# First edge pass of a graph network: 26 columns by one-hots and sixteen landed rows, in place of 34 and eight

## What is computed

```python
h = maximum(layernorm(x), 0)
nq = concatenate([h, query_embedding for every node], -1)
q, k = nq @ Wq + bq, nq @ Wk + bk
v = h @ Wv + bv
rel = relation_embeddings[edge_type]                 # 64 types
scores = sum(q[dst] * (k[src] + rel), over a head) / sqrt(16)
exp_s = exp(scores - max(segment_max(scores, dst), 0)[dst])
out = segment_sum(exp_s / (segment_sum(exp_s, dst) + 1e-8)[dst] * v[src], dst)
x = x + out @ Wo + bo
```

## Time and profile before

| | us |
|---|---|
| median of 3 runs | 8171.97 (8163.74 to 8175.19) |
| profiled execution | 8224.43 |
| its span | 8222.7 |
| first gather of the pass to last landed-value product | 1229.7 to 3020.07 |

### The profile page before, as it was taken

The page is one execution under the profiler, slowest core; times in us unless marked ns, Lnnn a source line. Parts: engine busy times, 40 slices in busy tenths (PEclk is TensorE's granted clock), DMA queues, the critical chain, the costliest instruction groups (busy, mean ns, idle before and its releaser), DMA issues. The chain is left out here.

```text
span 8222.7 us, 115102 instructions
## 1 busy us (share of the span) xinstructions
PE 3022.9 (37%) x29723; PEld 2454.6 (30%) x29724; DVE 4813.4 (59%) x11169; ACT 1435.3 (17%) x3773; POOL 3490.1 (42%) x3926
## 2 busy tenths in 40 slices
PE   4189423445566652244323432344300000001344
PEld 3178312344455542233223432333200000000122
DVE  9658835556566555677556875677544444444333
ACT  0123100111111121222112221344411111110000
POOL 0100113333323324456445653544466665563655
PEclk9999955667677675667666676666655555555666
DMA  0023203333323333334433453334322222222334
GB/s 20 10 85 100 51 27 100 80 92 88 85 69 83 77 60 68 79 80 87 64 75 80 82 82 61 72 80 72 57 48 53 52 52 50 46 50 54 78 82 78
DMA packets 297357, 557.19 MB, mean 68 GB/s; under 512 B 137694, under 2 KB 182475, under 8 KB 280515
## 3 DMA queue, kind: packets, MB, share of 16 engines
q0 software_dynamic: 112432, 254.18, 20.4%
q1 hardware_dynamic: 146802, 260.29, 10.0%
q10 hardware_dynamic: 38049, 41.86, 1.7%
HBM read 459.57 MB, written 29.32 MB: 59 GB/s over the span
## 5 line engine op out<-in xcount | busy, mean ns | idle before, releaser
L2967 PE MATMUL bank<-tab,oh 128*128 128x136 bf16 x11700 | 895.5, 249 | 695.4 <-PEq L2959 406.5
L2967 PEld LDWEIGHTS bank<-tab,oh 128*128 128x128 bf16 x11700 | 866.2, 112 | 755.5 <-issue 755.5
L1382 PE MATMUL bank<-ident,hid 128*128 128x128 f32 x125 | 55.8, 446 | 2651.0 <-PEq L1381 1182.8
L1382 PEld LDWEIGHTS bank<-ident,hid 128*128 128x128 f32 x125 | 22.7, 182 | 2697.7 <-issue 2697.7
L2710 POOL DMA_INDIRECT land_a<-table,idx_a x624 | 680.2, 1090 | 228.9 <-issue 166.4
L2729 POOL DMA_INDIRECT land_r<-table,idx_r x492 | 495.8, 1008 | 215.6 <-issue 144.4
L2546 PE MATMUL bank<-tab_l,oh_l 128*128 128x128 bf16 x3846 | 446.8, 243 | 289.2 <-issue 230.7
L2890 ACT ACTIVATE rows<-bank 128x408 f32<-128x408 f32 x936 | 398.5, 513 | 854.3 <-ACTq L2889 639.5
L2816 DVE TENSOR_TENSOR prod<-prod 128x128 f32<-128x128 f32 (+4 forms) x621 | 536.8, 864 | 14.6
L2519 PE MATMUL bank<-rel_l,oht_l 128*128 128x128 bf16 x3222 | 436.8, 261 | 245.4 <-issue 124.6
L2802 DVE TENSOR_TENSOR prod<-rows,bank 128x5376 f32<-128x5376 f32 x75 | 431.6, 5755 | 53.5 <-DVEq L2801 30.6
(11 more groups left out here) (506 smaller groups left out, 8264.3 us busy)
## 6 DMA issues: line engine op xcount, KB each, us to landing
loc<-el_loc SPq DMA_DIRECT2D x78, 1088.0 KB
loc_l<-el_loc SPq DMA_DIRECT2D x52, 1088.0 KB
rows_r<-land_r SPq DMA_DIRECT2D x123, 272.0 KB
landings_l<-landings_l SPq DMA_DIRECT2D x41, 784.0 KB
attr<-in_edge_attr ACTq DMA_DIRECT2D x75, 343.8 KB
land_a<-table,idx_a POOLq DMA_INDIRECT x936
typ_l<-el_typ SPq DMA_DIRECT2D x52, 192.0 KB
land_r<-table,idx_r POOLq DMA_INDIRECT x492
```

Source lines behind the costliest of these rows:

```text
L2967: last = pe.matmul(got[g % full][:, (c - of[0]) * W1:(c - of[0] + 1) * W1], oh[:, o], tab[:, t, x], start=n == 0, stop=n == len(parts) - 1 ...
```

## The change

The eight wide columns are no longer made by TensorE: their table rows, whose indices now stand in the stored list ahead of the overflow slots, are gathered by GpSimd. FC = 26 columns stay with the one-hots, LAND = 16 are landed. The key groups become four landed, two narrow of four columns and six narrow of three; the twelve value groups cover 26 columns in twos and threes. The relation types are loaded in two pieces in the order of the columns. The stored list is eight entries longer, and the later passes read it at an offset. The overflow turns keep their slots.

```diff
--- before
+++ after
@@ -148,7 +148,7 @@
-        el_ovf = dram("el_ovf", [RMAX + 1, P, 2 * LISTW], I32)
+        el_ovf = dram("el_ovf", [RMAX + 1, P, NW + 2 * LISTW], I32)
@@ -1249,7 +1249,7 @@
-                sp.dma_start(el_ovf[bass.ds(r + n, 1)].rearrange("r p s -> p (r s)"), ov_i[:, PC:]).then_inc(s("el_stored"), 16)
+                sp.dma_start(el_ovf[bass.ds(r + n, 1)].rearrange("r p s -> p (r s)"), ov_i[:, PC - NW:]).then_inc(s("el_stored"), 16)
@@ -2035,19 +2035,21 @@
-assert MC % 2 == 0
+FC = NB + 1
+LAND = MC - FC
+assert MC % 2 == 0 and LAND == NW + FIRST
...
-run_idx, run_now = bb("run_idx", [P, 2 * LISTW], I32), bb("run_now", [P, 2 * LISTW], I32)
-idx_a, idx_r = bb("idx_a", [P, FIRST], I32), bb("idx_r", [P, 2, MORE], I32)
-loc, typ = bb("loc", [P, PC * P], F16), bb("typ", [P, TH * P], F16)
-oh, oht = bb("oh", [P, OHC, P], BF16), bb("oht", [P, TH, P], BF16)
+run_idx, run_now = bb("run_idx", [P, NW + 2 * LISTW], I32), bb("run_now", [P, NW + 2 * LISTW], I32)
+idx_a, idx_r = bb("idx_a", [P, LAND], I32), bb("idx_r", [P, 2, MORE], I32)
+loc, typ = bb("loc", [P, FC * P], F16), bb("typ", [P, TH * P], F16)
+oh, oht = bb("oh", [P, FC, P], BF16), bb("oht", [P, TH, P], BF16)
...
-land_a, va = bb("land_a", [P, FIRST, W0]), bb("va", [P, FIRST, HV])
+land_a, va = bb("land_a", [P, LAND, W0]), bb("va", [P, LAND, HV])
@@ -2061,21 +2063,18 @@
-wide = [range(c, min(c + 4, PC)) for c in range(NB + 1, PC, 4)]
 narrow = [range(c, c + 4) for c in range(NB - 7, NB + 1, 4)] + [range(c, c + 3) for c in range(0, NB - 7, 3)]
-landed_groups = [range(PC + c, PC + c + HALF) for c in range(0, FIRST, HALF)]
-key_groups = landed_groups + wide + narrow
-value_groups = [range(max(c - BANKC, 0), c) for c in range(PC, 0, -BANKC)]
+landed_groups = [range(c, c + HALF) for c in range(FC, MC, HALF)]
+key_groups = landed_groups + narrow
+VG = 2 * len(banks)
+value_groups = [range(FC * (n - 1) // VG, FC * n // VG) for n in range(VG, 0, -1)]
 AHEAD = len(banks)
-type_halves = [[(9, 18), (30, MC)], [(0, 9), (18, 30)]]
-type_place = {}
-for k, pieces_of in enumerate(type_halves):
-    of_half = [c for a0, a1 in pieces_of for c in range(a0, a1)]
-    type_place.update({c: (k, i) for i, c in enumerate(of_half)})
+type_place = {c: (c // TH, c % TH) for c in range(MC)}
...
-assert sorted(c for of in value_groups for c in of) == list(range(PC))
+assert sorted(c for of in value_groups for c in of) == list(range(FC))
+assert all(len(of) <= BANKC for of in value_groups)
@@ -2105,14 +2104,12 @@
-            sp.dma_start(loc[:], el_loc[bass.ds(r, 1), 0:PC].rearrange("r j p -> (r j p)").partition_broadcast(P)).then_inc(s("loc_in"), 16)
+            sp.dma_start(loc[:], el_loc[bass.ds(r, 1), 0:FC].rearrange("r j p -> (r j p)").partition_broadcast(P)).then_inc(s("loc_in"), 16)
...
-            for k, pieces_of in enumerate(type_halves):
-                for a0, a1 in pieces_of:
-                    at = type_place[a0][1]
-                    sp.dma_start(typ[k * TYPES:(k + 1) * TYPES, at * P:(at + a1 - a0) * P],
-                                 el_typ[bass.ds(r, 1), a0:a1].rearrange("r j p -> (r j p)").partition_broadcast(TYPES)).then_inc(s("typ_in"), 16)
+            for k in range(2):
+                sp.dma_start(typ[k * TYPES:(k + 1) * TYPES],
+                             el_typ[bass.ds(r, 1), k * TH:(k + 1) * TH].rearrange("r j p -> (r j p)").partition_broadcast(TYPES)).then_inc(s("typ_in"), 16)
@@ -2158,9 +2155,9 @@
-            pool.tensor_copy(idx_a[:], run_idx[:, 0:FIRST]).then_inc(ch.semaphore, ch.one())
+            pool.tensor_copy(idx_a[:], run_idx[:, 0:LAND]).then_inc(ch.semaphore, ch.one())
             copied()
-            for c in range(FIRST):
+            for c in range(LAND):
@@ -2177,7 +2174,7 @@
-                    pool.tensor_copy(idx_r[:], run_now[:].rearrange("p (k s) -> p k s", k=2)[:, :, bass.ds(i * MORE + FIRST, MORE)]).then_inc(ch.semaphore, ch.one())
+                    pool.tensor_copy(idx_r[:], run_now[:, NW:].rearrange("p (k s) -> p k s", k=2)[:, :, bass.ds(i * MORE + FIRST, MORE)]).then_inc(ch.semaphore, ch.one())
@@ -2208,8 +2205,8 @@
-            dve.wait_ge(s("typ_in"), 64)
-            dve.sem_inc(s("typ_in"), -64)
+            dve.wait_ge(s("typ_in"), 32)
+            dve.sem_inc(s("typ_in"), -32)
@@ -2218,10 +2215,7 @@
-            dve.tensor_scalar(oh[:, 0:PC].rearrange("p c n -> p (c n)"), loc[:], iota_p[:], None, ALU.is_equal).then_inc(ch.semaphore, ch.one())
-            for k in range(1, WIDE):
-                dve.tensor_scalar(oh[:, PC + (k - 1) * NW:PC + k * NW].rearrange("p c n -> p (c n)"), loc[:, (NB + 1) * P:],
-                                  iota_k[:, k:k + 1], None, ALU.is_equal).then_inc(ch.semaphore, ch.one())
+            dve.tensor_scalar(oh[:].rearrange("p c n -> p (c n)"), loc[:], iota_p[:], None, ALU.is_equal).then_inc(ch.semaphore, ch.one())
@@ -2322,7 +2316,7 @@
-            dve.tensor_tensor(by_head(kp[:, PC:]), by_head(va[:]), wt[:, PC:MC].unsqueeze(3).broadcast_to([P, FIRST, HEADS, V]), ALU.mult).then_inc(ch.semaphore, ch.one())
+            dve.tensor_tensor(by_head(kp[:, FC:]), by_head(va[:]), wt[:, FC:MC].unsqueeze(3).broadcast_to([P, LAND, HEADS, V]), ALU.mult).then_inc(ch.semaphore, ch.one())
@@ -2406,7 +2400,7 @@
-            act.wait_ge(s("got_a_l0"), r * (16 * FIRST) + 16 * FIRST)
+            act.wait_ge(s("got_a_l0"), r * (16 * LAND) + 16 * LAND)
@@ -2522,22 +2516,22 @@
-                if of[0] >= PC:
+                if of[0] >= FC:
...
-                    done = pe.matmul(keys_of(n), ident[:], land_a[:, of[0] - PC:of[0] - PC + HALF, 0:D],
+                    done = pe.matmul(keys_of(n), ident[:], land_a[:, of[0] - FC:of[0] - FC + HALF, 0:D],
                                      start=False, stop=True, skip_group_check=True)
-                    if n == 1:
+                    if n == len(landed_groups) - 1:
...
-                        pe.sem_inc(s("bank_full1"), 1)
+                        pe.sem_inc(s(f"bank_full{n}"), 1)
                     else:
-                        done.then_inc(s("bank_full0"), 1)
+                        done.then_inc(s(f"bank_full{n}"), 1)
@@ -2647,7 +2641,7 @@
-            sp.dma_start(run_idx[:], el_ovf[bass.ds(r, 1), :, 0:LISTW].rearrange("r p s -> p (r s)")).then_inc(s("list_in"), 16)
+            sp.dma_start(run_idx[:], el_ovf[bass.ds(r, 1), :, NW:NW + LISTW].rearrange("r p s -> p (r s)")).then_inc(s("list_in"), 16)
```

## The result

After the change the kernel takes **8311.12 us** (median of 4 runs, 8294.45 to 8319.74), beside 8173.58 for the kernel before in the same series: ratio 1.0168, 95% interval 1.015 to 1.0186, slower by 137.5 us where I forecast 69. The profiled execution of after (8309.06, span 8307.3) lies at its median; that of before lay 52 above its own. The loss is in this pass.

A forecast was written before the change was run, and what follows sets the result against it. TensorE's issue was taken to be nearly stopped while gathers are in flight in the first edge pass. Fourteen single-turn intervals +21, two-turn +20, longer ones and the first +20, one more +8: +69 on 8172, 8241 us; range 8140 to 8320.

The forecast's parts named there:

- the pricing of the interval: First edge pass, per interval between landed-value products: +1.5 us with one overflow turn, +4 with two, +4 with three to five.
- 1.3 us of VectorE's time booked as saved: Behind the keys: VectorE's value groups take 4.3 us for 26 columns instead of 5.68 for 34.
- Rival A: First gathers do not lengthen TensorE's slow stretch; single-turn late keys end before 48.9; -209 us, 7963; chance 0.13.
- C: Late keys all pass at 3.6 per us and the values are covered: +5 us, no change; chance 0.14.
- D: As C, plus a stock of queued matmuls when the late keys start: -32 us, 8140; chance 0.07.
- B: The poorer pace, 0.9 matmuls per us, holds throughout the stretch under gathers: +151 us, 8323; chance 0.16.
- The pace of the late keys in the stretch: TensorE, single-turn interval: 3.6 per us under first gathers, 2.3 or 0.9 under overflow gathers, leaving 37 to 54 matmuls.
- The 2.5 us saved behind the keys: Single-turn interval after the last keys: 1.3 us from fewer value columns and 1.2 us from smaller one-hots.
- The longer intervals: Two-turn intervals: +4 us each, ends 0 and +8; the four longer ones and the first alike, +4 each.
- ScalarE's wait and copy, SyncE's loads and the later passes: ScalarE's wait for sixteen gathers, its doubled copy, and the loads are hidden: counted zero.

The follow-up runs named there:

- e1: Before with eight more gathers a run of the same table rows into a buffer nothing reads: 8438.83 us, ratio 1.033.
- e2: After without the eight gathers of the wide columns, their landed rows left at zero: 7991.92 us, ratio 0.9789.
- e3: After with value groups cut in another order, nine columns instead of thirteen in the last six groups: 8299.17 us, ratio 1.0161.
- e4: Before with probe stages behind the pass, 500 matmuls alone, beside loads and beside 24 gathers: 28.2 us beside loads, 58 us beside gathers.
- e8: Before with probe stages on burst length, wide matmuls and VectorE operations: 500 matmuls beside three bursts of eight gathers took 51 us, beside an unbroken burst 58.
- e11: Before, unchanged, paired with e12 in one ordinary series: 8213.3 us.
- e12: After, unchanged, in the same series as e11: 8344.56 us, ratio 1.016.
- e14: After, unchanged, in a quick series where before took 7532.15: 7675.31 us, ratio 1.0183.
- e13: After with a pause of three small memsets on GpSimd behind every fourth first gather and ahead of each overflow turn's eight, quick series: 7956.37 us.
- e9: After with pauses of six small memsets on GpSimd behind every fourth first gather and amid the turns' gathers, quick series: 8372.15 us.
- e10: Before with overflow gathers held back until the keys are made, plus the pauses of e9, quick series: 7885.26 us.
- e17: The same kernel as e13, in an ordinary series: 8197.08 us, ratio 1.0012.
- e18: Before, unchanged, in an ordinary series: 8190.55 us.

## Why the forecast was right and where it was wrong

**The step that failed** is the pricing of the interval: I took +1.5, +4 and +4 us for the single-turn, two-turn and longer intervals, and they cost +3.4, +6.3 and +7.4. Behind that stand a pace taken as constant where the runs show one that decays, and 1.3 us of VectorE's time booked as saved where the runs show TensorE's second half of the values setting the time.

**Direction, counts and the kind of mechanism** were right: the gathers hold TensorE's issue, a longer burst holds it longer, and e1 and e2 show both halves. Rival A (gathers do not lengthen the stretch) falls: the late keys end at 50.7, not before 48.9, and e1 lost 10 us an interval. A named the Trainium skill (Runtime: NRT & Kernel Launch, Instruction fetch mechanics), by which fetch is hidden behind the sequencer's issue. The traces bear that out: not one instruction packet from 1700 to 3130 us of after, where the stops are. What I drew from it for A does not follow: the stop is not fetch, and more gathers prolong it all the same (0.8 matmuls per us instead of 17.2 beside 24 of them). C (all at 3.6 per us) and D fall by the 13 matmuls in 19 us. **B**, the poorer pace throughout, gave 8323 and lies 12 us from the result; its interval (66.0) is 1.2 above the measured 64.8, mine (63.0) 1.8 below.

**The size was off by half, in these terms of the sum.** In the single-turn interval, seen from its start:

| | forecast | measured |
|---|---|---|
| landed groups end | 10.3 | 8.3 |
| first gather issued | 12.1 | 10.0 |
| last overflow gather issued | 43.6 | 39.9 |
| slow stretch ends | 46.4 | 45.0 |
| late matmuls left over then | 37 to 54 | 68 |
| keys end | 50.0 | 50.7 |
| behind the keys | 12.6 | 14.1 |
| interval | +1.5 | +3.4 |

The last three rows are cut as in the forecast. By the end of the last key matmul the same is +4.2 (46.9 to 51.1) for the keys and -0.8 (14.5 to 13.7) for what is behind them, where I forecast +3.6 and -2.5.

- *The pace of the late keys in the stretch.* I took averages of the earlier trace rows as if they were constants: 3.6 per us under first gathers, 2.3 or 0.9 under the turn's. They are means over matmuls that still pass quickly and a stop behind them. Ahead of the stop there passed 29 late ones here, and 11 in the 19 us of it (0.6 per us). Two more terms of mine were off and partly cancel, which is luck: the last overflow gather came 3.7 us earlier than forecast (39.9 against 43.6; the first gather at 10.0, and 1.28 us a gather instead of 1.39), and the stop lasted 5.1 us behind it instead of 2.8. So the stretch ended 1.4 early and hid half of the pace's error: the keys end only 0.7 late. In the two-turn intervals it shows whole: keys end 12 us later (about 62.8 against 50.6), not 10.5.
- *The 2.5 us saved behind the keys.* Here most of the single-turn error lies. 1.2 for the one-hots came (L2218 takes 1.08 where L2221 and L2223 took 2.22). The 1.3 for fewer value columns did not: the groups' products ran from 2612.1 to 2618.0, 5.9 us where twelve took 5.68. I set VectorE's share and forgot who delivers: 78 values are cut in two halves of 39, ahead of the second TensorE idles, and it comes back at a granted clock of 0.50, 39 in 5.1 us. Before, at 1.00, it made 104 matmuls in 5.9 us at this place. e3 confirms the term: with the larger groups made before the wait the products ran in 4.6 us, and what is behind the keys shrank by the missing 1.3. But its keys ended later, so that the order alone gives little back.
- *The longer intervals*: the first four cost 7.4 each and the two-turn ones 6.3, where I took 4 from between 0 and 8. I chose the lower half since 37 matmuls still passed under gathers in the earlier trace rows; those pass once, ahead of the stop.

In sum the intervals gave 27 + 12 + 14 + 2 more than forecast, by the table above, less 5 in the first: 50 of the missing 68.5. Nine or ten more are the reference: before's pass took 1686.0 in the execution that lay 52 above the median, and 1676.6 and 1677.6 in e4 and e8, whose first pass is before's, in series where before took 8170 and 8176. Against those after's 1805.0 is +128, as in the pair e11 and e12, not +119. The last eight or nine are not placed.

ScalarE's wait and copy, SyncE's loads and the later passes cost nothing, as said: ScalarE's doubled copy took 2.02 us under TensorE's landed groups.

## What to carry to other kernels

A gather by indirect DMA had two prices here: GpSimd's own (1.25 us) and the one that TensorE and VectorE, the two engines tried, pay beside it; the second grows with the length of the unbroken burst and can be the larger. Before trading matmuls for gathers, ask where the burst falls, and split it or move it to where the other engines wait anyway: the same gathers, held back until the keys were made, took 200 us from the kernel before. And a pace read from one window is a mean: read it in narrower windows before multiplying with it.

## What the runs showed of the hardware that I had not expected

- Beside an unbroken burst of 24 gathers, short matmuls fall from 17 per us to 0.8, after a stock of 61 to 84 at full pace; small VectorE operations fall from 12 to 1.4 per us (22 in 16.1 us). Four gathers cost nothing, SyncE's plain loads of 117 GB/s nothing, and rows of 64 bytes as much as long ones. The pace is back 2.5 us behind the issue of the last of eight gathers, 5 us behind the last of 24. In the stop both engines start again only at multiples of 0.70 us, in the kernel too (2582.86, 2585.65, 2588.45, 2591.25, 2593.36 in after). No instruction packets go with it. What links the gathers with the other engines' issue was not found.
- The stop comes and goes with something outside the program: in two of the seven series of the experiments before took 7532 and 7534 instead of 8170 to 8208, with TensorE at full pace beside gathers (e14). It is not simply the chip: the record gives chip 15 for e1 to e4 (8170) and for e13 and e14 (7532), chip 0 for e9 and e10 (7534) and for e17 and e18 (8186). So the same number stands on both sides; what changes is not known. What lies behind the three convolutions, whose code no kernel here changed, was 224 us shorter in e14 than in e12 (2107 and 2331, the same kernel). The ratio of the change was about the same, 1.0168 and 1.0183, though what bounds after differs.
- A gather that begins while VectorE runs one of its longest f32 products of two SBUF tiles is held: in e14 the two of 3.06 and 3.69 us began in the landed-value product (2.42 us from 2613.55) and in the halving sums (4.74 us from 2616.84). Over all traces 214 of the 230 gathers of the pass that began inside such a product of over 2 us took over 2 us themselves, and 6 of the 16362 others did. It is so in ordinary series too (43 of 47 in e17); in before and after no gather falls there. That the product holds the gather is read from this coincidence, no run moved the one and kept the other.
